# Two products over all 128 rows, with results that are thrown away, ahead of every burst of transposed scores in the first two of eight elements

## The reference

```python
h = _layernorm(x, ln1_g, ln1_b)
q = (h @ Wq).reshape(Bb, Ss, H, Dh)
k = (h @ Wk).reshape(Bb, Ss, H, Dh)
v = (h @ Wv).reshape(Bb, Ss, H, Dh)
scores = jnp.einsum('bqhd,bkhd->bhqk', q, k) / jnp.sqrt(jnp.float32(Dh))
attn = jax.nn.softmax(scores, axis=-1)
ctx = jnp.einsum('bhqk,bkhd->bqhd', attn, v).reshape(Bb, Ss, Dd)
```

## Time and profile before

| | |
|---|---|
| time, median of 3 runs | 1064.16 us (1063.0 to 1066.33) |
| the profiled execution: time, span | 1063.83 us, 1061.8 us |
| granted TensorE clock over the span | 0.862 |
| busy: PE, PEld, DVE, ACT, POOL | 830.0, 512.3, 658.8, 589.1, 422.5 us |
| first and last burst of transposed scores start | 104.0, 908.6 us |

### The profile page before, as it was taken

The page is one execution under the profiler, slowest core; times in us unless marked ns, Lnnn a source line. Parts: engine busy times, 40 slices in busy tenths (PEclk is TensorE's granted clock), DMA queues, the critical chain, the costliest instruction groups (busy, mean ns, idle before and its releaser), DMA issues. The chain is left out here.

```text
span 1061.8 us, 15480 instructions
## 1 busy us (share of the span) xinstructions
PE 830.0 (78%) x5245; PEld 512.3 (48%) x5245; DVE 658.8 (62%) x1331; ACT 589.1 (55%) x984; POOL 422.5 (40%) x545
## 2 busy tenths in 40 slices
PE   2166888778877888999998899889988898747760
PEld 1143445344434445555556455655554555546760
DVE  3528757875787677867876798589665673211101
ACT  1123455535643568768766877687667777423330
POOL 4454215325522543264327336843260370035005
PEclk9576797768766889999989999899899999977885
DMA  6400231990000042232213223405132352538742
GB/s 194 126 10 1 90 99 46 292 288 30 1 1 1 30 149 83 84 112 84 82 58 103 90 83 108 137 16 160 58 102 80 100 156 78 166 127 266 228 151 59
DMA packets 99164, 109.59 MB, mean 103 GB/s; under 512 B 7647, under 2 KB 83086, under 8 KB 99086
## 3 DMA queue, kind: packets, MB, share of 16 engines
q1 hardware_dynamic: 94990, 100.20, 30.1%
q0 software_dynamic: 4096, 8.40, 2.4%
HBM read 72.63 MB, written 35.93 MB: 102 GB/s over the span
## 5 line engine op out<-in xcount | busy, mean ns | idle before, releaser
L1380 DVE TENSOR_REDUCE QA<-psB 128x2 f32<-128x1024 f32 x256 | 312.0, 1219 | 153.1 <-PE psB L1076 152.2
L894 ACT ACTIVATE PT<-psB 128x1024 f32<-128x1024 f32 x256 | 261.8, 1023 | 146.3 <-PE psB L1092 145.5
L1076 PE MATMUL psB<-KT,Q 24*128 24x512 f32 x512 | 140.4, 543 | 31.4 <-DVE QA L1380 30.8
L1092 PE MATMUL psB<-Q,KT 32*128 32x512 f32 x512 | 136.4, 529 | 30.7 <-ACT PT L894 24.2
L1104 PE MATMUL psV<-PT,VA 128*32 128x512 f32 x1024 | 157.3, 690 | 0.4
L1169 PE MATMUL psA<-MX,WB 128*128 128x128 f32 x736 | 107.9, 305 | 22.7 <-ACT H L922 17.3
L922 ACT ACTIVATE H<-psA,WB 128x128 f32<-128x128 f32 x368 | 102.3, 377 | 28.4 <-PE psA L1169 27.9
L1092 PEld LDWEIGHTS psB<-Q,KT 32*128 32x128 f32 x512 | 50.4, 193 | 133.8 <-ACT PT L894 79.5
L1169 PEld LDWEIGHTS psA<-MX,WB 128*128 128x128 f32 x736 | 100.3, 217 | 30.0 <-issue 16.5
L1179 PE MATMUL psY<-WB,H 128*128 128x128 f32 x736 | 99.1, 282 | 0.7 <-ACT H L922 0.7
L1179 PEld LDWEIGHTS psY<-WB,H 128*128 128x128 f32 x736 | 89.2, 193 | 19.4 <-issue 14.0
(11 more groups left out here) (195 smaller groups left out, 1340.7 us busy)
## 6 DMA issues: line engine op xcount, KB each, us to landing
WB<-w_rows SPq DMA_DIRECT2D x92, 578.0 KB, 5.0
pairs<-XT SPq DMA_DIRECT2D x2, 4608.0 KB, 16.9
outs<-XT SPq DMA_DIRECT2D x2, 4608.0 KB, 30.1
XT<-pairs SPq DMA_DIRECT2D x92, 64.0 KB
outs<-YT SPq DMA_DIRECT2D x92, 64.0 KB
w_rows<-WB SPq DMA_DIRECT2D x8, 578.0 KB, 3.1
X<-in_L_attn_x_dram SPq DMA_DIRECT2D x8, 256.0 KB, 2.9
H<-in_L_ffn_W_dram SPq DMA_DIRECT2D x8, 256.0 KB, 4.2
```

The lines of the kernel that those rows point to most:

```text
L894: act.activation(PT[:, (c % 2) * G + j:(c % 2) * G + j + 2, :], psT, ACT.Exp, scale=SCALE).then_inc(t_taken.sem, 1)
L1076: pe.matmul(psS[:, h, :], chunk(Q1[r, g, :], c), KT[r, g, :], start=True, stop=True).then_inc(s_full.sem, 1)
L1092: pe.matmul(psT[:, h, :], chunk(KT[r, g, :], c), Q2[r, g % 2, :], start=True, stop=True).then_inc(t_full.sem, 1)
L1380: dve.tensor_reduce(QA[:, c, g * G + j:g * G + j + 2, RM], psS, AX_X, ALU.max).then_inc(s_taken.sem, 1)
```

## The change

Ahead of the two products of `score_t`, and behind its waits, PE now issues two further products in elements 0 and 1: all 128 rows of a 128-column chunk of `KT` as weights, against all 512 columns of `KT` of the same group of heads. Both go to the first bank of `psT` and are overwritten by the burst that follows. There are 2 x 32 x 2 = 128 of them. Only PE's list is longer; the lists of the other engines are the same apart from line numbers, and no semaphore is added.

```diff
+            EXTRA = 2
+
             def score_t(b, i):
                 g, c, j = i // 8, i // 2 % NT, 2 * i % G
                 if i % 8 == 0:
                     pe.wait_ge(use(b, f"q2_{g}").taken, use(b, f"q2_{g}").after)
                 if b + i > 0:
                     pe.wait_ge(t_taken.sem, t_taken.at(b, i))
+                for _ in range(EXTRA if b < 2 else 0):
+                    pe.matmul(psT[:, 0, :], chunk(KT[:, g, :], c), KT[:, g, :], start=True, stop=True)
                 for h in range(2):
                     r = slice((j + h) * HW, (j + h + 1) * HW)
                     pe.matmul(psT[:, h, :], chunk(KT[r, g, :], c), Q2[r, g % 2, :],
```

## The result

The changed kernel takes 1071.57 us (median of 20 runs) against 1066.07 for the kernel before (20 runs); the ratio is 1.0057 with a 95% interval of 1.0039 to 1.0076, so it is slower by 4 to 8 us. The profiled execution takes 1069.18 us (span 1067.2), 5.35 above the one of before.

A forecast was written before the change was run, and what follows sets the result against it. PE's in-order list was taken to set the pace, with exceptions, slowed by the clock in elements 0 and 1. +40.3 - 9 - 23.5 + 5.6 = +13.4 us on 1063.83 gave 1077 us, own range 1068 to 1088.

The forecast's parts named there:

- The price of a pair: Ahead of each burst in elements 0 and 1: two added products take 0.63 us at full clock, 1.13 at half.
- The time at the lower level: Elements 0 and 1: time at the lower clock level falls from 94 us to 38 us.
- two bounds: Lower-level time left in elements 0 and 1: 94 us if none goes, 14 us if as in elements 3 to 5.
- A bare step pays in full: Steps holding nothing else, elements 0 and 1: the next Exp starts later by the whole pair, 1.64 to 2.27 us.
- "All 64 bursts pay", less 9 us: Elements 0 and 1: 64 pairs at 0.63 add 40.3 us; later asking hides 9 us of waits.
- What the clock gives back: Elements 0 and 1: less time at the lower level saves 23.5 us, (94 - 38) / 2 x 0.84.
- the dearer pairs: Pairs in the 38 us left at the lower level of elements 0 and 1 cost 1.13 each, adding 5.6 us.
- Sum: Whole kernel: +40.3 - 9 - 23.5 + 5.6 = +13.4 us, giving 1077 us; elements 2 to 7 only start later.
- the level one: Rival, elements 0 and 1: pair price 0.63, clock as in elements 3 to 5, sum 0, 1064 us; chance 0.15.
- third: Rival, elements 0 and 1: each product stands alone, 0.86 us a pair, +28.5 us, 1092 us; chance 0.13.
- fourth: Rival, elements 0 and 1: clock does not rise, 94 us stay at half, +46 us, 1110 us; chance 0.05.
- The first: Rival, elements 0 and 1: clock pays for more than it costs, faster, around 1055 us; chance 0.22.

The follow-up runs named there:

- e5: Pair behind both kinds of scores, not ahead of the burst, 480 columns, 56 of 64 steps of elements 0 and 1; ratio 1.0047 to the kernel before.
- e1: Same pair ahead of every burst, but in elements 3 and 4 instead of 0 and 1; 1086.16 us, ratio 1.0214 to the kernel before.
- e6: No pairs; 93 single products of 128 rows ahead of waiting instructions in elements 1 and 2; ratio 0.9865 to the kernel before.
- e2: Changed kernel's pair in elements 0 and 1 with the same columns on 32 rows, not 128; 1094.40 us, ratio 1.0285 to the kernel before.
- e7: No pairs; 93 single products of 32 rows ahead of waiting instructions in elements 1 and 2; ratio 1.0030 to the kernel before.
- e3: Changed kernel with one added product per burst in place of two, elements 0 and 1; 1063.24 us, ratio 0.9988 to the kernel before.

## Why the prediction came out as it did

It forecast 1077 us, +13, for a measured +5.5 to +6. The direction, the range and the order of the mechanism (the pairs cost more than the clock gives back) are right, and the size is twice too large: elements 0 and 1 take 208.9 us together, not the 217 that it named as its sign. By its own steps:

- **The price of a pair: right.** 0.63 forecast, 0.66 measured; 0.335 us from the first product to the second (0.30 forecast) and 0.327 to the burst (0.33). At the lower level 1.13 was forecast and 1.13 measured (4 pairs). The Trainium skill says ("TensorE: Matmul & The Clock Gate", Part 3, "What overlaps and what doesn't") that a weight load overlaps running products only where the row group differs. By that the pair would take 0.86, and the trace disagrees: both loads, to the same 128 rows, are done within 0.30 us.
- **The time at the lower level: right.** 38 us forecast, 38 measured, mean clock 0.91 forecast, 0.93 and 0.89 measured. That it is so near is luck, since I placed it between two bounds.
- **A bare step pays in full: right.** 2.27 forecast, 2.31 measured; e5 shows that it is the place ahead of the burst that makes it so.
- **"All 64 bursts pay", less 9 us: the step that failed.** Net price 40.3 - 9 = 31 us forecast; e1 measured 19.0 in elements 3 and 4, or 20.5 with its own gain of clock (14 to 9 us at the lower level) added back. I read what could be hidden from the list of waits, and that part came as forecast: the waits for DVE and for EE in the earlier trace rows fell from 20.1 to 11.1 us. The lag of 14 us was there in the start times, in part behind a running burst, and the joint (some 28 bursts stand right behind a product of 128 rows without a wait; at 0.17 to 0.20 us some 5 us) stood in the timeline one row behind the earlier trace rows, where a burst follows the 16 products. I used the 16 products for the pair but did not look at what happens where such products meet a burst. 42.2 - 14.0 - 5 - 2 for the other waits of DVE is 21.
- **What the clock gives back: 18 us forecast, 13 to 18 found.** (94 - 38) / 2 x 0.84 = 23.5, less 5.6 for the dearer pairs, was the forecast. The runs give 0.23 (e6), 0.27 and 0.32 (e2) and 0.30 us (e7) for each us at the lower level, so 56 us are worth 13 to 18, with the dearer pairs in it; the runs do not fix it more closely. I had 0.42 before the dearer pairs, as if PE set the pace whenever it was busy and its work always took twice as long. From a burst to the next row it is 0.43 us at the higher level and 0.72 at the lower (166.17 to 166.89), not 0.86. The stretches of the earlier trace rows spoke for less too: steps 16 to 19 took 14.50 us at 0.76 and 13.40 at 1.00 with 2.3 us more of PE work. A faster PE reaches the next chain sooner and waits. That these are the whole reason was not tested.
- **Sum.** 20.5 less 13 to 18 is +2.5 to +7.5, against +5.3 in the two elements. This checks the account, but not closely: the 20.5 is from other elements, and 0.27 would give +5.5.

Of the rivals, the level one had the clock higher than it came; the third and fourth are refuted by the timeline and by the clock. The first named 0.46 us a pair as the price from which the clock pays, with 9 us hidden; the pair came at 0.66, but far more of it was hidden. Net of the covers a pair costs 0.32, and the clock gives back 0.20 to 0.28 for each. With one product in place of two (e3) they come out even.

## What to carry to other kernels

Work that is added to hold the clock is free only where the engine waits, or where what follows is late anyway, so put it in the waits and not ahead of the work: 93 products in the waits of elements 1 and 2 made the kernel 1.3 to 1.8% faster, 128 ahead of the bursts of elements 0 and 1 made it 0.6% slower. To price an added instruction, look at the start times around it, not only at the idle times: an instruction that starts late behind a running one is cover too. And check a filler against one with fewer rows in use, to know that the clock is what it buys.

## What the runs showed of the hardware that I had not expected

- Products of 32 rows do not hold the clock, even at 92% busy time (e7: 0.82 and 0.84); the same columns on 128 rows in the same places do (e6: 1.00 and 0.95).
- Going from products of 128 rows to products of 32 rows costs 0.17 us: behind the 16 products of 128 rows, an added product of 128 rows starts 0.17 us earlier than the burst on two strips of rows did, and one of 32 rows (e2) starts no earlier.
- Products on different strips of rows do not keep the order of the list: in e2 the burst's other product and the scores start 0.01 us behind the first added product, and the second added one, which stands ahead of them in the list, 0.34 behind it.
- The clock fell in element 1 of the kernel before around waits of at most 2.6 us, and in e6 stayed up with waits of 0.7 us (for the context) and 1.6 us (for the rows) left in that element.
